# Two loops of one kernel: routing weights spread by repeating transfers instead of products, and the second loop's preparation moved ahead with its z products in four banks

## The reference, cut to what matters

```python
# layer 0, feed-forward: w[t, e] is zero but for the 4 chosen experts of a token
hid = silu(tokens @ gate_w[e].T) * (tokens @ up_w[e].T)      # per expert e, 64 wide
out = sum_e (hid * w[:, e]) @ down_w[e].T  +  shared expert
```

```python
mixed = silu(causal_dwconv(concat(q, k, v), conv_w))
S = S*exp(g); delta = (v - k@S)*beta; S = S + k^T delta; o = q@S     # step by step over the tokens
core = rms(o) * gate_norm_w * silu(z)
```

## Time and profile before

| what | value |
|---|---|
| median of 3 runs | 3129.29 us (3120.68 to 3132.71) |
| the profiled execution | 3119.86 us, span 3118.1 us |
| busy PE / DVE / ACT / POOL | 2659.2 (85%) / 2023.4 (65%) / 1196.5 (38%) / 354.3 (11%) us |
| mean granted TensorE clock | 0.899 of full speed |
| DMA | 110.69 MB, 36 GB/s in the mean |
| chain that ended last | PE 54%, issue 17%, DVE 15%, ACT 5%, DMA 5%, SP's queue 2% |

### The profile page before, as it was taken

One profiled execution on the slowest core, in us unless ns is written; L12 is line 12 of the kernel. 1 busy time (PEld: TensorE's weight loads), 2 busy tenths in 40 slices (PEclk: granted clock), 3 DMA queues, 4 the chain that ended last, 5 costly groups with the idle time before them and its releaser, 6 DMA issues.

```text
span 3118.1 us, 48104 instructions
## 1 busy us (share of the span) xinstructions
PE 2659.2 (85%) x15020; PEld 1784.9 (57%) x15020; DVE 2023.4 (65%) x6343; ACT 1196.5 (38%) x2194; POOL 354.3 (11%) x284
## 2 busy tenths in 40 slices
PE   2888888888888886898798798799799799799798
PEld 1434343343434434585596596596496497487587
DVE  4757576575757656557657657657657746846855
ACT  0132231313222134445445446445445445444444
POOL 0000000000000001022022021120220221211211
PEclk8888888897888977899999999899999999899899
DMA  5010201102020112101101201201201101110110
GB/s 141 9 38 7 32 12 28 30 9 38 7 32 12 28 28 59 52 8 52 59 6 50 62 1 55 62 2 55 56 8 55 46 17 53 37 28 29 54 35 28
DMA packets 133983, 110.69 MB, mean 36 GB/s; under 512 B 77000, under 2 KB 117520, under 8 KB 133232
## 3 DMA queue, kind: packets, MB, share of 16 engines
q1 hardware_dynamic: 130480, 101.06, 12.9%
q10 hardware_dynamic: 3264, 6.82, 0.6%
HBM read 87.67 MB, written 20.19 MB: 35 GB/s over the span
## 4 chain that ended last, share of the span: by engine, by line
PE 54%; issue 17%; DVE 15%; ACT 5%; DMA 5%; SPq 2%; POOL 1%; ACTq 0%; DVEq 0%; POOLq 0%
PE bank L887 5%; PE bank L877 5%; PE bank L471 5%; DMA arena<-scrk 4%; DVE arena L1567 3%; DVE arena L1625 3%; DVE arena L1623 2%; PE bank L827 2%; PE bank L622 2%; PE bank L567 2%; PE bank L790 2%; PE bank L785 2%; PE bank L773 2%; PE bank L777 2%; PE bank L552 2%
## 5 line engine op out<-in xcount | busy, mean ns | idle before, releaser
L887 PEld LDWEIGHTS bank<-wring,arena 128*128 128x128 f32 x2048 | 281.9, 203 | 171.9 <-issue 121.7
L887 PE MATMUL bank<-wring,arena 128*128 128x128 f32 x2048 | 288.5, 289 | 65.0 <-ACT arena L1121 44.4
L877 PE MATMUL bank<-arena,wring 128*128 128x512 f32 x512 | 297.5, 668 | 34.5 <-ACT arena L1121 34.5
L1121 ACT ACTIVATE arena<-bank,w_b 128x512 f32<-128x512 f32 x256 | 175.1, 687 | 388.1 <-PE bank L877 387.6
L995 ACT ACTIVATE arena<-bank 128x512 f32<-128x512 f32 x136 | 81.4, 598 | 503.4 <-PE bank L552 445.1
L1567 DVE SCALAR_TENSOR_TENSOR arena<-bank,w_convw,arena 128x511 f32<-128x511 f32 (+2 forms) x384 | 255.0, 738 | 14.4 <-ACT arena L1035 14.3
L1411 DVE CUSTOM_DVE_ANT_0 bank<-bank,arena 128x128 f32<-128x128 f32 (+3 forms) x512 | 249.2, 492 | 0.0
L471 PE MATMUL bank<-w_ident,arena 128*128 128x128 f32 (+2 forms) x1164 | 175.3, 290 | 85.9 <-DVE arena L1305 35.6
L1004 ACT ACTIVATE arena<-bank 128x512 f32<-128x512 f32 (+1 forms) x384 | 171.1, 535 | 146.8 <-PE bank L609 145.2
L471 PEld LDWEIGHTS bank<-w_ident,arena 128*128 128x128 f32 (+2 forms) x1164 | 137.1, 141 | 115.8 <-issue 65.1
L1087 ACT ACTIVATE arena<-bank 128x512 f32<-128x512 f32 (+1 forms) x256 | 118.7, 487 | 139.4 <-PE bank L785 69.1
(11 more groups left out here) (274 smaller groups left out, 5102.4 us busy)
## 6 DMA issues: line engine op xcount, KB each, us to landing
wring<-in_w_last SPq DMA_DIRECT2D x66, 512.0 KB, 3.3
arena<-scrg SPq DMA_DIRECT2D x32, 512.0 KB, 5.5
arena<-scrq SPq DMA_DIRECT2D x108, 64.0 KB
arena<-scrk SPq DMA_DIRECT2D x108, 64.0 KB
scrn<-arena SPq DMA_DIRECT2D x64, 64.0 KB, 1.9
arena<-scrn SPq DMA_DIRECT2D x8, 512.0 KB, 3.9
scrx<-arena SPq DMA_DIRECT2D x8, 512.0 KB, 3.2
arena<-scrx SPq DMA_DIRECT2D x64, 64.0 KB, 2.1
```

The costliest lines, as they stand in the source:

```text
L877: mm(bank[HBANK[f]][:, :], wring[:, e % 2, k * P:(k + 1) * P], xn1T, start=True, stop=True).then_inc(*s["p_fh"].up)
L887: last = mm(bank[OBANK[e]][:, t * P:(t + 1) * P], GH[:, f % 2, t * P:(t + 1) * P], wring[:, e % 2, FC * P + k * D:FC * P + (k + 1) * D], s ...
L1121: fn(GH[:, f % 2, :], bank[HBANK[f]][:, :], ACT.Gelu_apprx_tanh, bias=W["b1"][:, f:f + 1]).then_inc(*s["a_gh"].up)
```

## The change

1. First loop: `spread`, `sel0` and `W96` go. `fw` on DVE is one copy (L1381) into `wt`, and it moves from group 2, item 11 to item 3. SP writes `wt` to DRAM (`weights_out`) and reads each row back 64 times over (`weights_in`), two transfers of 64 partitions by 2 KB for each `p`, into seven slots `WB`. `hid` reads its slot and waits for the slot's transfer. Slots 0 and 1 are read ahead of `scratch_in`, slots 2 to 6 at the head of the next turn, and the others as slots come free. Ahead of the loop the order on SP is the same: `scratch_out`, the first weights, `scratch_in`.
2. Second loop: `gam` goes ahead of `qkv(10)`, the four `prep` steps stand closer together and fh, gelu and fo behind them; `cz` is split in PE's part `cz` and ACT's part `sz`; the z products use banks 0 and 1, 2 and 3, 0 and 1, 4 and 5 (`ZBANK`), so that two chunks stand at a time. `cz(2)` and `cz(3)` go to PE ahead of two expert steps; `cv(0)` and `wfT` go behind the first four stages of the inverse. ACT's turn now ends at `("silu", 8)`.

```diff
-             (2, 11): [("fw",)]}
+             (2, 3): [("fw",)]}
...
+WSLOTS = 7
+ZBANK = (0, 2, 0, 4)
...
-    order += [("taps", 6), ("ssq", 2), ("qkv", 8), ("silu", 6), ("ssq", 4), ("ssq", 6), ("qkv", 10), ("scan", 0), ("stat",), ("scan", 1)]
-    order += [("fh", 2), ("gam",), ("prep", 0), ("gelu", 2), ("fo", 2), ("fh", 3), ("prep", 1), ("gelu", 3), ("fo", 3), ("fh", 4)]
-    order += [("prep", 2), ("gelu", 4), ("fh", 5), ("prep", 3), ("gelu", 5), ("rr",), ("facc", 0), ("fo", 4), ("fo", 5), ("taps", 8)]
-    order += [("fh", 6), ("gelu", 6), ("fh", 7), ("gelu", 7), ("taps", 10), ("silu", 8), ("qkv", 12), ("fo", 6), ("taps", 12)]
-    order += [("silu", 10), ("qkv", 14), ("fo", 7), ("taps", 14), ("silu", 12), ("silu", 14)]
-    order += [("cz", 0), ("fh", 8), ("cz", 1), ("gelu", 8), ("sub", 0)]
+    order += [("taps", 6), ("ssq", 2), ("qkv", 8), ("silu", 6), ("ssq", 4), ("ssq", 6), ("scan", 0), ("stat",), ("scan", 1), ("gam",)]
+    order += [("fh", 2), ("qkv", 10), ("prep", 0), ("gelu", 2), ("prep", 1), ("fo", 2), ("fh", 3), ("prep", 2), ("gelu", 3), ("fo", 3)]
+    order += [("fh", 4), ("prep", 3), ("gelu", 4), ("rr",), ("facc", 0), ("fh", 5), ("gelu", 5), ("fo", 4), ("taps", 8), ("fh", 6)]
+    order += [("fo", 5), ("gelu", 6), ("fh", 7), ("fo", 6), ("gelu", 7), ("taps", 10), ("silu", 8), ("qkv", 12), ("fo", 7), ("taps", 12)]
+    order += [("silu", 10), ("qkv", 14), ("taps", 14), ("cz", 0), ("cz", 1), ("silu", 12), ("silu", 14), ("sz", 0), ("sz", 1)]
+    order += [("fh", 8), ("gelu", 8), ("sub", 0)]
...
-    order += [("sub", 3), ("facc", 3), ("stat2",)] + ffn(1) + [("cz", 2), ("cz", 3), ("cv", 0)] + ffn(1) + ffn_rest() + [("wfT",), ("facc", 4)]
+    order += [("sub", 3), ("cz", 2), ("cz", 3), ("facc", 3), ("stat2",)] + ffn(2) + ffn_rest() + [("sz", 2), ("sz", 3), ("facc", 4)]
-    order += steps(0, 0, 1, 2, 3)
+    order += steps(0, 0, 1, 2, 3) + [("cv", 0), ("wfT",)]
...
+            def weights_in(p, b, k):
+                if p == 0:
+                    sp_.wait_ge(*s["d_ws"].at(b, 16, k))
+                elif p >= WSLOTS:
+                    sp_.wait_ge(*s["v_hid"].at(b, p - WSLOTS + 1, k))
+                for hh in range(2):
+                    part = bass.AP(tensor=scrw.tensor, offset=(2 * p + hh) * S, ap=[[0, 64], [1, S]])
+                    sp_.dma_start(WB[64 * hh:64 * hh + 64, p % WSLOTS, :], part).then_inc(*s[f"d_wb{p % WSLOTS}"].up16)
...
-            ahead_of_loop(scratch_out, scratch_in)
+            ahead_of_loop(scratch_out, first_weights, scratch_in)
...
-                    if p > 1:
-                        spread(p - 1)
...
-                        bk = after(*(("a_sz", 2 * c - 1 + i) if c else ("v_prep", 2 * NT - 1 + i)), i)
+                        bk = after(*(("v_prep", 2 * NT - 1 + i), ("v_cv", NQKV - 3 + i), ("a_sz", 1 + i), ("v_cv", NQKV - 1 + i))[c],
+                                   ZBANK[c] + i)
...
-            turn = L1.index(("gelu", 6))
+            turn = L1.index(("silu", 8))
...
-                link(v.tensor_copy(wt, bank[4][0:E0, :]))
-                split_rows(link, wt, wtr, wtm, W96, E0).then_inc(*s["v_w96"].up)
+                v.tensor_copy(wt, bank[4][0:E0, :]).then_inc(*s["v_wt"].up)
...
-                    dve.wait_ge(*s["p_wb"].at(b, p + 1, k))
-                    v.tensor_tensor(HID[:, p % 2, :], HDT[:, p % 2, :], bank[4 + 2 * (p % 2)][:, :], ALU.mult
+                    dve.wait_ge(*s[f"d_wb{p % WSLOTS}"].at(b, 32 * (p // WSLOTS + 1), k))
+                    v.tensor_tensor(HID[:, p % 2, :], HDT[:, p % 2, :], WB[:, p % WSLOTS, :], ALU.mult
```

More of the change, by code:

```diff
@@ L48 @@
     "ident": ([P, P], F32), "identb": ([P, P], BF16), "maskq": ([P, S], F32), "maskt": ([P, P], BF16),
-    "grank": ([P, 2, NT, G0, G0], F32), "sel0": ([96, PR0, P], BF16),
+    "grank": ([P, 2, NT, G0, G0], F32),
     "gate0": ([D, PR0, P], F32), "up0": ([D, PR0, P], F32), "down0": ([P, PR0, D], F32),
@@ L182, in build @@
 def build(nc, x_in, w_last, out, weights, scratch, per, sizes):
-    scrq, scrk, scrm, mid, scrg, scrn, scrx = scratch
+    scrq, scrk, scrm, mid, scrg, scrn, scrx, scrw = scratch
     x_v = x_in.rearrange("b (t p) d -> b p t d", p=P)
@@ L246, in build @@
         x = cut([NT, D]); xr = cut([NT, D])
-        W96 = cut([S], BF16, parts=96)
+        WB = cut([WSLOTS, S])
         xn = cut([NT, D]); xnT = cut([S]); qf = cut([S]); qf2 = cut([S]); kf = cut([S]); kf2 = cut([S])
@@ L259, in build @@
         qs3 = cut([3, S], BF16); ks3 = cut([3, S], BF16)
-        wt = cut([S], parts=E0); wtm = cut([S], BF16, parts=E0); wtr = cut([S], parts=E0)
+        wt = cut([S], parts=E0)
         rden, att = qf, qf2
@@ L366, in scratch_out, with weights_out, first_weights @@
                 sp_.dma_start(planes(scrk, 2, 3), ks3[:, 2:3, :]).then_inc(*s["d_scrk"].up16)
+            def weights_out(b, k):
+                sp_.wait_ge(*s["v_wt"].at(b, 1, k))
+                sp_.dma_start(scrw, wt).then_inc(*s["d_ws"].up16)
+            def weights_in(p, b, k):
[6 more added lines that the diff above has]
+                    sp_.dma_start(WB[64 * hh:64 * hh + 64, p % WSLOTS, :], part).then_inc(*s[f"d_wb{p % WSLOTS}"].up16)
+            def first_weights(b, k):
+                weights_out(b, k)
+                for p in range(2):
+                    weights_in(p, b, k)
             def scratch_in(b, k):
@@ L381, in _ @@
             sp_.wait_ge(s["g_init"].sem, 3)
-            ahead_of_loop(scratch_out, scratch_in)
+            ahead_of_loop(scratch_out, first_weights, scratch_in)
             with sp_.Fori(0, LOOPS) as b:
+                for p in range(2, WSLOTS):
+                    weights_in(p, b, 0)
                 sp_.wait_ge(*s["a_xr"].at(b, 1))
@@ L386, in _ @@
                               ).then_inc(*s["x_in"].up16)
+                for p in range(WSLOTS, PR0):
+                    weights_in(p, b, 0)
                 for half, landed in enumerate(("d_m", "d_m2")):
@@ L403, in _ @@
             sp_.wait_ge(*s["x_in"].at(LOOPS, 16))
+            for p in range(2):
+                sp_.wait_ge(*s[f"d_wb{p}"].at(LOOPS, 32))
             sp_.dma_start(x1[:, :, :], mid_v[0]).then_inc(s["d_x1"].sem, 16)
@@ L537, in _ @@
                 pe.wait_ge(*s["a_xnT"].at(b, 1))
[L539 to L544, removed]
                 def gu(p):
@@ L556, in gu @@
                        ).then_inc(*s["p_up"].up)
-                    if p == 1:
-                        pe.wait_ge(*s["v_w96"].at(b, 1))
-                        spread(0)
                 def wbd(p):
@@ L713, in wfT_ @@
                     pe.wait_ge(*s["v_wf"].at(b, 1, late))
-                    bk = after("a_sz", 2 * NT - 1, 0)
+                    bk = after("a_sz", 5, 0)
                     for t in range(NT):
@@ L751, in cv @@
                     for i in range(2):
-                        bk = after(*(("v_o", 2 * c - 1 + i) if c else ("v_cv", NQKV - 1 + i)), 4 + i)
+                        bk = after(*(("v_o", 2 * c - 1 + i) if c else ("a_sz", 2 * NT - 1 + i)), 4 + i)
                         for h in range(4):
@@ L824, in sdl @@
                         need(f"v_inv{i}", INV_V * (c + 1))
-                        bk = after(*(("v_R", 2 * (c - 1) + i + 1) if c else (("v_wfT", 1), ("a_sz", 2 * NT))[i]), i)
+                        bk = after(*(("v_R", 2 * (c - 1) + i + 1) if c else (("v_wfT", 1), ("a_sz", 6))[i]), i)
                         for j in range(4):
@@ L1060, in cz @@
                         act.wait_ge(*s["p_z"].at(b, 2 * c + i + 1, late))
-                        fn(sz(c)[:, 4 * i:4 * i + 4, :].rearrange("p a b -> p (a b)"), bank[i][:, :], ACT.Silu
+                        fn(sz(c)[:, 4 * i:4 * i + 4, :].rearrange("p a b -> p (a b)"), bank[ZBANK[c] + i][:, :], ACT.Silu
                            ).then_inc(*s["a_sz"].up)
@@ L1132, in moe1 @@
                     fn(SG1[:, p % 2, :], bank[1 + p % 2][:, :], ACT.Silu).then_inc(*s["a_sg1"].up)
-                return {"qkv": qkv, "silu": silu, "gam": gam, "cz": cz, "cv": cv, "inv": inv, "so1": so1, "sdl": sdl,
+                return {"qkv": qkv, "silu": silu, "gam": gam, "sz": cz, "cv": cv, "inv": inv, "so1": so1, "sdl": sdl,
                          "ct": ct, "gelu": ffn, "h4": h4, "moe1": moe1, "gT": lambda: gT(b, late + 1),
                          "gfe": lambda: gfe(b, late + 1), "gab": lambda: gab(b, late + 1)}
-            turn = L1.index(("gelu", 6))
+            turn = L1.index(("silu", 8))
             def first_part(b, k):
@@ L1241, in _ @@
             v = nc.vector
-            for buf, value in ((W96, 0.0), (W96b, 0.0), (nhalf, -0.5), (top4, PAD), (top2, PAD),
+            for buf, value in ((W96b, 0.0), (nhalf, -0.5), (top4, PAD), (top2, PAD),
                                (tmp36, PAD), (pad8, PAD)):
@@ L1848, in sel @@
         return a
-    c["sel0"], c["sel1"] = sel(E0, PR0), sel(E1, PR1)
+    c["sel1"] = sel(E1, PR1)
     c["upto"], c["after"], c["ones"] = (i <= j), (i > j), np.ones((P, P))
```

19 lines of the change are left out of this document (10 added, 9 removed).

## The result

| | before | after |
|---|---|---|
| median | 3128.62 us (4 runs, 3120.68 to 3132.71) | 3054.02 us (4 runs, 3050.35 to 3063.34) |
| ratio | | 0.977, 95% interval 0.9744 to 0.9797 |
| profiled execution, span | 3119.86, 3118.1 us | 3055.48, 3053.7 us |
| from the first reload to the ninth, first loop | 61.29 to 1151.01 | 72.86 to 1153.83 |
| last `mid` issued, first loop | 1166.78 | 1168.29 |

The kernel is 2.3% faster. Against the profiled run 64.4 us are gone, where the forecast had 81. The first loop is 1.5 us longer (to the last `mid`), and all that follows it 65.9 us shorter. Turns are counted from 0 in both loops. In what follows a mean turn of the second loop is that of the seven intervals between eight transfers out of `sub` (before 1289.62 to 2971.86, after 1280.76 to 2910.08).

What follows compares the result with a forecast made beforehand. PE, the fullest engine in both loops (83%, 89%), was taken as the bound through its idle and half-clock stretches. First loop 14 plus second loop 67 made 81 us off 3119.9, 3039; median said 3043, range 3010 to 3085.

Steps and rivals of the forecast that it cites:

- The 11 us ahead of the loop: Before the first loop: first reload waits behind the weights' way out, 72.4 instead of 61.29; 11 us lost, once.
- The six pairs: First loop, gate steps: twelve of the sixteen removed spreads, 0.23 us gained per pair, 1.4 us a turn.
- Two lie at half clock ... 2 x 0.46 = 0.9 us: First loop: two removed spreads, behind the reload wait and behind fnorm, where DVE waits for PE; 0.9 us gained a turn.
- they give nothing: First loop: two removed spreads ahead of the reload wait gain 0, since the reloads start from the last score and cover them.
- `fw` (0.8): First loop: moving fw earlier takes about 1.0 us off the path to pv(1); 0.8 us gained a turn, bounds 0 and 1.0.
- POOL, at 1.00 us each ... ends at about 1704.7: Second loop, preparation: POOL's eight scalings end at about 1704.7 instead of 1710.1; the preparation was to gain 6.8 us.
- I take 2.4, with 0 and 2.95 as bounds: Second loop: ACT's jump, now between gelu 7 and silu 8 on the path to taps(12), takes 2.4 us.
- The 4.3 to be given back: Second loop, inverse starting 12.4 us earlier: lost again 1.3 us for transposes, 1.7 for clock, 1.3 for gelu 20's table load.
- rival B: ACT's jump is free and PE is never slowed ahead of the inverse: about 3005 to 3020 us; chance 0.16.
- C: Only one second-loop part, preparation or z products, comes through: about 4 us a turn, 3078 us; chance 0.19.
- D: The time stays, 3105 to 3135 us, both chains closed again by something late such as weights from DRAM; chance 0.04.
- E: Slower: the wait ahead of the inverse leaves the clock low far longer, 3159 us at 30 us more a turn; chance 0.05.

Runs made afterwards that it cites:

- two_slots: The kernel after without the weight transfers for p of 2 to 15, slots 0 and 1 used in turn instead (output differs): 3059.93 us, ratio 0.9783.
- fw_back: act_turn with fw moved back to group 2, item 11: 3029.32 us, ratio 0.9683.
- filled6: The kernel after with six unused f32 products on PE ahead of its wait for the reloads in the first loop: 3044.77 us, ratio 0.9735.
- act_turn: The kernel after with ACT's turn ending ahead of gelu 6 again instead of at silu 8: 3030.01 us, ratio 0.9677.
- inv_filled: act_turn plus three unused f32 products on PE ahead of its wait for the inverse's operands: 3030.67 us, ratio 0.9674.
- pool_late: act_turn with POOL's eight scalings waiting until the last exponential is done, so beside no scan: 3023.07 us, ratio 0.9684.
- filled: The kernel after with four unused f32 products on PE ahead of its wait for the reloads in the first loop: 3049.18 us, ratio 0.9746.
- best6: The kernel after with the edits of act_turn and filled6, and the reloads issued before the first weights ahead of the loop: 3015.75 us, ratio 0.9636.
- all_filled: best6 plus the edit of inv_filled: 3011.34 us, ratio 0.9624.

## Why the prediction came out, point by point

The total was right, 3054 against 3043 and inside the range. The terms were not all. The first loop gave nothing of its 14 us, and that is what the time lacks; that the second loop's total agrees to 1 us is luck, since two errors in it cancelled. Two of the prediction's own signs of being wrong came: ACT's jump was longer than DVE's, and the clock fell in other places than before. Of its turns, 232 us came in the second loop (232.8), and 133 did not in the first (136.6).

*First loop, forecast +14, measured -1.5.* The 11 us ahead of the loop came as worked out (first reload at 72.86, forecast 72.4; 11.6 us). Reload to first `max` stayed at 25.8. The six pairs gave about what was said: two steps in 7.36 us (509.59 to 516.95; forecast 7.2 to 7.4), 0.5 us from `hid(3)` to `hid(9)` and 0.5 from `hid(10)` to `hid(15)`, 1.0 of 1.4. The weights' transfers cost nothing (`two_slots`). What failed is the step "Two lie at half clock ... 2 x 0.46 = 0.9 us", and with it "they give nothing" for the two spreads ahead of the wait. Less than nothing came of the work taken away there: it became idle time, PE waited 4.4 us, and the clock was low earlier and longer. The spreads are the smaller share of it (0.4 us); the larger is that PE's work behind the last score ran at full clock, which `fw_back` puts down to the move of `fw`. From the first `max` to `hid(3)` 1.2 us are lost instead of 0.5 gained. `filled6` shows that the idle time is the cause: without it the same stretch takes 8.5 us. The other term that failed is `fw` (0.8). Its stretch, from the keys' way out to the first reload, did get shorter, 18.8 us in the mean of eight turns instead of 19.5, but `fw_back` shows 0 in the time. The long low clock of the attention is as long as before, 20.5 us (in the turn shown from 76.3 to 96.7 us behind the first `max` before, from 77.9 to 98.4 after). In the steady turns all of this adds up to 0 (136.6 us before and after); the turns gave 8.7 us in all instead of 25, and a sum over one execution is no closer than the 15 us by which like loops differ. The forecast's upper bound of 31 is also mis-added: its own terms make 4.7 us a turn, not 5. It changed nothing.

*Second loop, forecast 67, measured 66.* A mean turn is 7.6 us shorter, forecast 8.1. From the first scan to the way out of `sub` it gained 1.9 us (76.8 to 74.9, the mean of the last seven turns) where I had 5.3:
- The preparation ends 25.5 us behind the first scan in the mean instead of 29.7: 4.2 us, forecast 6.8. The step "POOL, at 1.00 us each ... ends at about 1704.7" is wrong. It took the price of a scaling from a stretch in which POOL ran alone. Beside scans it is 1.44, and the scans are slower too. That is 3.5 us on POOL and 2.4 on DVE. DVE's share is what the preparation waited for: in the turn shown it starts the first `prep` right behind the last scan, 12.1 us behind the first (1685.51), forecast 10.1. The four then take 13.6 us instead of 12.2, since DVE waits 3.6 us for PE's products in them and not 2.2.
- The jump: "I take 2.4, with 0 and 2.95 as bounds". The six jumps took 4.48, 4.16, 3.67, 2.27, 4.35 and 2.13 us, 21.1 together and 3.5 in the mean, beyond my upper bound. There are six, not seven. `act_turn` gives this back, 24 us in the medians. With it the mechanism is shown, and its size was off.

*From the way out to the next scan* it gained 5.7 us (163.5 to 157.9), where the forecast leaves 12.4 - 5.3 - 4.3 = 2.8. The start of the inverse came 7.2 us closer to the way out (15.7 to 8.5), as worked out. The 4.3 to be given back was too much. The table load ahead of gelu 20 costs nothing: it is loaded at 1838.91 and done at 1840.19, and the product that gelu 20 waits for starts at 1841.56; ACT had been idle there before. The 1.7 us of clock at the inverse are there, 3.63 against 2.01, but filling the wait moved them on (`inv_filled`). Before, the clock also fell twice in the same stretch, 5.0 and 25.4 us behind the way out of the turn shown. In all, 1.5 of the 7.2 us were given back.

Half of rival B is in `act_turn`: the jump is out of the way, the clock still falls, and the time is 3030. C did not hold: the two parts give 50 us each and add up. D did not: `hid` waited for its weights once, 1.74 us in the first turn. E did not: behind the wait the clock is low for 3.4 to 6.8 us, as the nearest rows had it.

## What to carry to other kernels

Taking work away in front of a wait that a transfer ends gained nothing here, and it lost 1.2 us behind the wait: PE idled longer and ran its next products at half clock. Look first at what PE does in that wait. A loop's backward jump has to lie where its engine is idle for longer than the jump takes, here up to 4.5 us, and every re-ordering has to be followed by the question where the jump now stands. A duration taken from a row holds for the neighbours that it had there.

## What the runs showed of the hardware

*Instruction fetch beside data.* The two jumps of ACT that took 2.27 and 2.13 us began within 0.2 us of SP's issue of the first expert weights. The four of 3.67 to 4.48 us began 0.6 to 1.8 us after that issue. Windows at one of each kind (last columns: DMA share and GB/s): in the jump of 4.16 us from 1706.43, then the 2 us up to the start of that of 2.27 us from 2174.83, and the 2 us in it:

```profile
1706.60:1708.60 2.00, 2.00 (x9) 1.04 (x9) 1.42 (x3) 0.00 (x0) 0.00 (x0) 1.00 0.94 377
...
2173.10:2175.10 2.00, 2.00 (x11) 1.44 (x12) 2.00 (x4) 0.69 (x1) 0.00 (x0) 1.00 0.02 2
2175.10:2177.10 2.00, 2.00 (x10) 1.13 (x8) 2.00 (x4) 0.00 (x1) 0.00 (x0) 1.00 0.96 242
```

The short jump starts in a quiet moment, but the transfers run beside the rest of it; over a whole jump they move 210 to 267 GB/s in all six, the short ones included. PE's jump ahead of `cz(0)` speaks against a simple rule: PE stood idle there for 0.84 us with 384 GB/s beside it (1710.9), and for 3.80 us with 109 (2179.3). That the transfers are what lengthens ACT's jump is a guess from these six starts. It was not tried and stays open. The page of the profile counts instruction fetches as DMA queues of their own:

```profile
q8 instruction: 104, 1.70, 0.2%
q14 instruction: 136, 1.11, 0.1%
```

The Trainium skill ("Runtime: NRT & Kernel Launch", section "Instruction fetch mechanics") says that a taken branch outside the window waits for a DMA fetch; by that rule the jump would cost, and the traces agree, with 2.1 to 4.5 us on ACT.

*DVE and POOL.* A scan alone took 1.14 us from start to start (4.56/4), a scaling alone 1.00; beside each other they come in pairs of up to 1.92 us, a little less than the two durations one after the other. Both read two operands from SBUF. The Trainium skill ("SBUF — State Buffer", section "Who interferes with whom") says that a DVE instruction with two SBUF inputs contends with a GpSimd instruction that reads SBUF; `pool_late` agrees. Whether they run side by side or apart can't be told in the time here (3030 and 3023 us).

*The clock.* Which stretch runs at half clock changes with small idle times elsewhere: in `filled` and `best6`, from turn 1 on, 0.7 to 1.6 us of idle time ahead of the first `max` went with turns of 136 to 137 us, and none with 133 to 135. It is not the whole of it: in `all_filled` a turn without idle time there took 135.9 us, with 9.7 us around `fnorm`.
